# Scores and output projection of a gated cross-attention layer: three fp32r products each, or one plain fp32 product

## The chip, the cores and the metric

The kernel runs on one core of one Trainium2 chip. The metric is the device time of one execution in microseconds (us). All engines of the core run their own instruction streams and meet at semaphores: TensorE (PE in the profile, its weight loads PEld), VectorE (DVE), ScalarE (ACT), GpSimd (POOL) and SyncE (SP, which only issues transfers here).

## The reference, cut to what matters

Sixteen sequences of 256 tokens (width 256) attend to themselves and to 77 context rows, through 16 heads of 64; then comes a feed-forward part with a router, 15 experts and a shared branch.

```python
def xattn(image_embeds, latents, ...):            # x is (16, 256, 256), the context (16, 77, 256)
    x = layer_norm(image_embeds, ln1_g, ln1_b)
    l = layer_norm(latents, ln2_g, ln2_b)
    q = l @ Wq                                    # 256 x 1024
    k, v = split(concatenate([x, l], 1) @ Wkv)    # 333 keys per sequence
    w = softmax(einsum('bhqd,bhkd->bhqk', q * scale, k * scale))
    out = einsum('bhqk,bhkd->bhqd', w, v)
    return merge_heads(out) @ Wo                  # 1024 x 256
x = x + tanh(g_xattn[0]) * xattn(ctx_1024, layernorm(x), ...)
x = x + tanh(g_ffn[0]) * ffn(layernorm(x), ...)   # router top 2 of 16, experts, a causal convolution
```

## The kernel before

**Steps.** Attention is a software pipeline of 128 steps, 8 pairs of heads (`PAIRS`) in each of 16 sequences (`B`). A step `u` of sequence `b` does on TensorE, in this order: the scores of the pair of one step ago (`LAG_S`, L1396), probabilities times values of the pair of three steps ago (L1415), the projections of this pair's queries and keys (L1350, "Q" and "K"), the transposes of the normalised probabilities of two steps ago for the first two key tiles (`turned`, L1380), in six of eight steps one sixth of the value projection (L1350, "V", 512 columns), the third `turned`, in two of eight steps the transposes of the next sequence's rows (L1360, "L"), now and then work of the router, and the output projection of the pair of three steps ago (L1476), which adds up in the bank `yb` over eight pairs. Steps 0 to 31 and the last 16 are written out; the 80 between are a hardware loop of 16 steps, run five times (`pipeline`). The last sequences' router work, the shared branch and the experts follow, all of it in plain fp32.

**Precision.** Where a product must be as exact as fp32, the projections and two more products are made of three fp32r products: each operand is held as its rounded value and the rest (`Q_hl`, `K_hl`, `OT_hl`, `wo`, with an index of 0 or 1 for the two), and high times high, high times low and low times high are added in PSUM. The scores (L1396) and the output projection (L1476) are such products. Probabilities times values, all transposes and the feed-forward part are plain fp32 matmuls. The projections stay as they are in the change.

**Who makes the halves.** ScalarE copies a result bank to the rounded half (`Q_hl` at L1172, `K_hl` at L1180, `OT_hl` at L1168) and signals `q_hi`, `k_hi` or `ot_hi`; VectorE waits for that, subtracts and writes the other half (L1322, L1327, L1317), and it is this that releases the bank (`pj_free`) or tells TensorE (`ot_lo`). VectorE does this after the reciprocal of the sums (L1313), which waits for the fourth exponential, and before it copies two transposed tiles out of `st` (L1334, signal `pt_lo`). ScalarE copies the third (L1191, `pt_hi`). The scores need `pt_lo` and `pt_hi` of the step before, since they write the same `st` banks.

**Banks.** Q, K, V and L results take turns in two PSUM banks, `pj0` and `pj1`. So V, coming two fills after Q, goes into Q's bank and waits until that has been read.

**Output weights.** `Wo` is loaded to `stage` in two halves, each after one piece of the query weights has been split; in step 2 ScalarE copies (L1176) and GpSimd subtracts (L1100) to make `wo`. GpSimd's normalisation of probabilities (L1105, L1108) stands behind that in its stream.

**Shapes.** The scores take 64 rows: the two heads of a pair lie on partitions 0 to 63 and 64 to 127 and write different banks (`st_bank(2 * qt + head)`).

Of the kernel before, what the change touches and what calls it, by code (L numbers as in the profile page):

```python
# [587 lines left out]
def attention(nc, c, X, ident, tanh_g, kept, x, ctx_in, g_xattn, g_ffn, ln1_g, ln1_b, ln2_g, ln2_b,  # L588
# [53 lines left out]
    K_hl = sb("K_hl", [P, 2, 2, SKVE], F32R)  # L642
    Q_hl = sb("Q_hl", [P, 2, 2, SQ], F32R)
# [6 lines left out]
    OT_hl = sb("OT_hl", [P, 2, 2, SQ], F32R)  # L650
# [29 lines left out]
    with ExitStack() as weights:  # L680
        wq = weights.enter_context(nc.sbuf_tensor("wq", [P, 2, KD, INNER], F32R))
        wkv = weights.enter_context(nc.sbuf_tensor("wkv", [P, 2, KD, 2 * INNER], F32R))
        wo = weights.enter_context(nc.sbuf_tensor("wo", [P, 2, PAIRS, D], F32R))
# [13 lines left out]
    wo_in = [sem("wo_in0"), sem("wo_in1")]  # L697
    wo_hi = sem("wo_hi")
    wo_split = sem("wo_split")
# [15 lines left out]
    q_hi = sem("q_hi")  # L715
    k_hi = sem("k_hi")
# [9 lines left out]
    ot_hi = sem("ot_hi")  # L726
    ot_lo = sem("ot_lo")
# [53 lines left out]
    def st_bank(i):  # L781

        return st[i // 2][:, i % 2]
# [22 lines left out]

    def wo_half(i):
        return slice(i * PAIRS // 2, (i + 1) * PAIRS // 2)

    def wo_stage(i):  # L810
        return stage[:, i, :].rearrange("p (q d) -> p q d", d=D)
# [214 lines left out]
    def sync(sp):  # L1026
# [12 lines left out]
        for i in range(2):  # L1039
            sp.wait_ge(w_lo, i + 1)  # L1040
            sp.dma_start(wo_stage(i), Wo.rearrange("(q p) d -> p q d", p=P)[:, wo_half(i), :]
                         ).then_inc(wo_in[i], 16)
        sp.wait_ge(zeros_set, 3)

        def step(bb, u, has):
# [8 lines left out]
            if isinstance(bb, int) and bb == 0 and u == 4:  # L1054
                sp.wait_ge(wo_split, 2)
# [12 lines left out]
    def gpsimd(pool):  # L1068
# [22 lines left out]
        def step(bb, u, has):  # L1091
# [5 lines left out]
            if isinstance(bb, int) and bb == 0 and u == 2:  # L1097
                for i in range(2):
                    pool.wait_ge(wo_hi, i + 1)
                    pool.tensor_tensor(wo[:, 1, wo_half(i), :], wo_stage(i), wo[:, 0, wo_half(i), :].bitcast(F32),  # L1100
                                       ALU.subtract).then_inc(wo_split, 1)
# [36 lines left out]
    def scalar(act):  # L1138
# [13 lines left out]
        def step(bb, u, has):  # L1152
# [10 lines left out]
            if has(LAG_AV):  # L1163
# [4 lines left out]
                copy(OT_hl[:, v, 0, :], ov[:, 0:SQ], ACT.Copy).then_inc(ot_hi, 1)  # L1168
            if has(0):
                n, bank, _, _ = filled("Q", PAIRS, bb, u)  # L1170
                act.wait_ge(pj_full, n + 1)
                copy(Q_hl[:, r, 0, :], bank[:, 0:SQ], ACT.Copy, scale=SCALE).then_inc(q_hi, 1)  # L1172
            if isinstance(bb, int) and bb == 0 and u == 2:
                for i in range(2):
                    act.wait_ge(wo_in[i], 16)
                    copy(wo[:, 0, wo_half(i), :], wo_stage(i), ACT.Copy).then_inc(wo_hi, 1)  # L1176
            if has(0):
                n, bank, _, _ = filled("K", PAIRS, bb, u)
                act.wait_ge(pj_full, n + 1)
                copy(K_hl[:, r, 0, :], bank[:, 0:SKVE], ACT.Copy).then_inc(k_hi, 1)  # L1180
# [19 lines left out]
    def vector(dve):  # L1200
# [86 lines left out]
        def step(bb, u, has):  # L1287
# [26 lines left out]
            if has(LAG_AV):  # L1314
                m, v = PAIRS * bb + u - LAG_AV, (u - LAG_AV) % 2
                dve.wait_ge(ot_hi, m + 1)
                tt(OT_hl[:, v, 1, :], ov[:, 0:SQ], OT_hl[:, v, 0, :].bitcast(F32), ALU.subtract  # L1317
                   ).then_inc(ot_lo, 1)
            if has(0):
                _, bank, free, _ = filled("Q", PAIRS, bb, u)  # L1320
                dve.wait_ge(q_hi, PAIRS * bb + u + 1)
                nc.vector.scalar_tensor_tensor(Q_hl[:, r, 1, :], bank[:, 0:SQ], SCALE,  # L1322
                                               Q_hl[:, r, 0, :].bitcast(F32), ALU.mult, ALU.subtract
                                               ).then_inc(free, 1)
# [193 lines left out]
```

## Time and profile before

| what | value |
|---|---|
| three timed runs | 1327.8, 1330.31, 3483.99 us, median 1330.31 |
| profiled execution | 1328.71 us, span from first to last instruction 1327.0 us |
| mean granted TensorE clock | 0.990 |
| TensorE matmul / weight load busy | 1248.6 us (94%) / 1017.4 us (77%) |
| VectorE busy | 878.3 us (66%) |
| GpSimd busy | 740.0 us (56%) |
| ScalarE busy | 666.0 us (50%) |

The busy time of TensorE counts each matmul from its start to the modelled end of its pipeline, so consecutive matmuls overlap, and a short wait is hidden in it. What a matmul costs in a row of others is therefore read from start to start. A plain fp32 matmul leaves two records in the trace, an fp32r matmul and a transpose one. In the timeline, one row merges consecutive records of one group: its first number is the start of the first, its second the time to the last modelled end.

### The profile page before, as it was taken

Reading aid. Unit: us, or ns where it says so; the run is one execution under the profiler, and the core shown is the slowest. Engines: PE = TensorE matmul, PEld = TensorE weight load, DVE = VectorE, ACT = ScalarE, POOL = GpSimd, SP = SyncE. Lnnn points to the kernel's source line nnn. Section 1 sums busy time; section 2 is a strip of 40 time slices with the busy share of each in tenths; the row PEclk is TensorE's granted clock in tenths of the full one; section 3 lists DMA queues with packets and bytes.
Section 4 is the critical chain, followed back from the end, with each engine's and each line's share of the span. In section 5 each row is a group of like instructions: output and inputs, shape, how many; then the busy total and the mean of one; then the engine's idle time right before and its main releaser. Section 6 shows DMA issues by size and latency. Waiting matters only on the chain.

```text
span 1327.0 us, 28196 instructions
## 1 busy us (share of the span) xinstructions
PE 1248.6 (94%) x8982; PEld 1017.4 (77%) x8982; DVE 878.3 (66%) x2646; ACT 666.0 (50%) x2022; POOL 740.0 (56%) x894
## 2 busy tenths in 40 slices
PE   3899999999999999899999998999999989999996
PEld 2688787878787878788878787878788878787774
DVE  5566677777776777777767776777766656434554
ACT  3555555555544455455544554455545566454442
POOL 2655545656664666566646665666565642344555
PEclk9999999999998999999989999999999999999998
DMA  8910000000000000000000000000000070445666
GB/s 258 314 32 1 3 1 3 17 4 18 4 17 5 17 4 18 5 18 4 17 5 17 4 18 5 17 4 18 1 17 1 17 194 29 120 126 174 186 215 207
DMA packets 61839, 70.90 MB, mean 53 GB/s; under 512 B 7072, under 2 KB 56176, under 8 KB 61680
## 3 DMA queue, kind: packets, MB, share of 16 engines
q1 hardware_dynamic: 54192, 48.91, 12.7%
q0 software_dynamic: 6912, 18.95, 4.0%
q8 instruction: 84, 1.38, 0.5%
q10 hardware_dynamic: 576, 1.05, 0.2%
q14 instruction: 75, 0.61, 0.2%
HBM read 35.19 MB, written 33.70 MB: 52 GB/s over the span
## 4 chain that ended last, share of the span: by engine, by line
PE 37%; POOL 29%; issue 24%; DVE 6%; DMA 2%; ACT 1%; POOLq 0%; SPq 0%; DVEq 0%; ACTq 0%
POOL probs L1108 19%; PE pj L1350 9%; PE st L560 5%; PE ov L1415 4%; PE st L1396 4%; PE st L1380 4%; POOL probs L1105 3%; POOL slots_x L982 3%; PE pj L513 3%; PE ov L579 2%; PE yb L1476 2%; POOL rstd L1088 1%; PE st L550 1%; PE pj L516 1%; DVE PT L1334 1%
## 5 line engine op out<-in xcount | busy, mean ns | idle before, releaser
L1108 POOL TENSOR_SCALAR probs<-probs,inv_sum 128x333 f32<-128x333 f32 x384 | 425.7, 1125 | 0.0
L1160 ACT ACTIVATE probs<-st,neg_max 128x333 f32<-128x333 f32 x512 | 268.8, 538 | 275.0 <-DVE neg_max L1302 275.0
L1105 POOL TENSOR_TENSOR probs<-probs,inv_sum 128x333 f32<-128x333 f32 x128 | 94.8, 741 | 407.9 <-DVE inv_sum L1313 407.7
L1302 DVE TENSOR_REDUCE neg_max<-st 128x2 f32<-128x666 f32 x256 | 205.9, 846 | 134.6 <-PE st L1396 134.6
L1380 PE MATMUL st<-ident,probs 128*128 128x128 f32 (+1 forms) x1536 | 203.8, 272 | 1.1 <-POOL probs L1108 1.1
L1415 PE MATMUL ov<-PT,V 128*64 128x256 f32 (+1 forms) x1536 | 196.9, 392 | 0.0
L1380 PEld LDWEIGHTS st<-ident,probs 128*128 128x128 f32 (+1 forms) x1536 | 182.5, 143 | 17.3 <-POOL probs L1108 1.4
L1396 PE MATMUL st<-K_hl,Q_hl 64*128 64x334 f32 x1536 | 154.1, 332 | 19.0 <-issue 9.5
L1350 PE MATMUL pj<-wkv,lT 128*128 128x512 f32 (+1 forms) x576 | 158.4, 410 | 13.4 <-DVE Q_hl L1322 13.3
L1334 DVE COPY PT<-st 128x512 f32<-128x512 f32 x256 | 163.7, 681 | 0.8 <-PE st L1380 0.8
L1186 ACT ACTIVATE V<-pj 128x512 f32<-128x512 f32 (+1 forms) x96 | 57.3, 596 | 192.8 <-PE pj L1350 192.8
L1396 PEld LDWEIGHTS st<-K_hl,Q_hl 64*128 64x128 f32 x1536 | 119.7, 188 | 39.6 <-issue 24.2
L1415 PEld LDWEIGHTS ov<-PT,V 128*64 128x64 f32 (+1 forms) x1536 | 99.9, 138 | 64.5 <-issue 28.1
L1350 PE MATMUL pj<-lT,wkv 128*128 128x334 f32 x768 | 140.6, 319 | 0.6 <-DVE wkv L1275 0.6
L1350 PEld LDWEIGHTS pj<-lT,wq 128*128 128x128 f32 x768 | 100.7, 191 | 52.6 <-issue 49.3
L1350 PE MATMUL pj<-lT,wq 128*128 128x256 f32 x768 | 127.8, 302 | 3.0 <-DVE lT L1262 3.0
L1350 PEld LDWEIGHTS pj<-wkv,lT 128*128 128x128 f32 (+1 forms) x576 | 93.6, 175 | 47.5 <-DVE Q_hl L1322 20.3
L1476 PE MATMUL yb<-wo,OT_hl 128*128 128x256 f32 x768 | 122.5, 295 | 0.5 <-DVE OT_hl L1317 0.5
L1350 PEld LDWEIGHTS pj<-lT,wkv 128*128 128x128 f32 x768 | 119.5, 191 | 0.9 <-DVE wkv L1275 0.9
L1160 ACT ACTIVATION_READ_ACCUMULATOR probs<-st,neg_max 128x1 f32 x512 | 103.8, 203 | 0.0
L1476 PEld LDWEIGHTS yb<-wo,OT_hl 128*128 128x128 f32 x768 | 99.6, 190 | 0.8 <-DVE OT_hl L1317 0.8
L1191 ACT ACTIVATE PT<-st 77x512 f32<-77x512 f32 x128 | 75.1, 587 | 29.5 <-PE st L1380 29.5
(176 smaller groups left out, 1722.0 us busy)
## 6 DMA issues: line engine op xcount, KB each, us to landing
slots_x<-zeros SPq DMA_DIRECT2D x10, 1032.0 KB, 13.0
V<-slots_x SPq DMA_DIRECT2D x80, 129.0 KB
yg<-routed_y SPq DMA_DIRECT2D x32, 256.0 KB, 3.5
out<-X SPq DMA_DIRECT2D x32, 128.0 KB
X<-in_x SPq DMA_DIRECT2D x2, 1024.0 KB, 14.7
w_gu<-in_L_ffn_expert_gate_w SPq DMA_DIRECT2D x2, 960.0 KB, 9.1
w_gu<-in_L_ffn_expert_up_w SPq DMA_DIRECT2D x2, 960.0 KB, 10.3
w_dn<-in_L_ffn_expert_down_w SPq DMA_DIRECT2D x1, 1920.0 KB, 12.7
```

Source lines behind the costliest of these rows:

```text
L560: last = nc.tensor.matmul(pg[m % 2], xT[:, m % 2, k * P:(k + 1) * P], w_gu[:, bass.ds(e, 1), k].rearrange("p a g i -> p (a g i)"), start=( ...
L1105: pool.tensor_tensor(probs[:, v, 0, 0:SKV], probs[:, v, 0, 0:SKV], inv_sum[:, v, 0:1].to_broadcast([P, SKV]), ALU.mult).then_inc(normed, 1)
L1108: pool.tensor_scalar(probs[:, v, i, 0:SKV], probs[:, v, i, 0:SKV], inv_sum[:, v, i:i + 1], None, ALU.mult).then_inc(normed, 1)
L1160: nc.scalar.activation(probs[:, v, i, 0:SKV], st_bank(i)[:, 0:SKV], ACT.Exp, bias=neg_max[:, v, i:i + 1], accum_out=sums[:, v, i:i + 1]).t ...
L1191: copy(PT[0:kn, v, 2, :], st_bank(2)[0:kn, :], ACT.Copy).then_inc(pt_hi, 1)
L1302: nc.vector.tensor_reduce(neg_max[:, v, 2 * i:2 * i + 2], st[i][:, :, 0:SKV], AX.X, ALU.max, negate=True).then_inc(maxed, 1)
L1334: nc.vector.tensor_copy(PT[:, v, kt, :], st_bank(kt)).then_inc(pt_lo, 1)
L1350: last = mm(out, lhs(a, k), rhs(r, k), start=(k == 0 and i == 0), stop=(k == KD - 1 and i == 2))
L1380: last = nc.tensor.transpose(st_bank(kt)[0:kn, at:at + P], probs[:, v, i, k0:k0 + kn], ident[:])
L1396: last = mm(st_bank(2 * qt + head)[:, 0:SKVE], Q_hl[own, r, a, qt * P:(qt + 1) * P], K_hl[own, r, a_, :], start=(n == 0), stop=(n == 2))
L1415: last = mm(ov[half * HALF:(half + 1) * HALF, 0:SQ], V[0:kn, kt, head * DH:(head + 1) * DH], PT[0:kn, v, kt, half * SQ:(half + 1) * SQ], s ...
L1476: last = mm(yb[:, t * D:(t + 1) * D], OT_hl[:, v, a, t * P:(t + 1) * P], wo[:, r_, q, :], start=(q == 0 and t == 0 and i == 0), stop=(q == ...
```

## The change

Scores and output projection become single plain fp32 matmuls. `Q_hl`, `K_hl` and `OT_hl` become `Q`, `K` and `OT`, one fp32 value each. ScalarE copies Q (with the scale) and OT, and its Q copy releases the bank; VectorE copies K straight from the bank and releases it. The subtractions and ScalarE's K copy are gone. `wo` is one tile that one transfer of 1 MB fills, issued without a wait; the copies and subtractions of step 2 are gone.

```diff
-    K_hl = sb("K_hl", [P, 2, 2, SKVE], F32R)
-    Q_hl = sb("Q_hl", [P, 2, 2, SQ], F32R)
+    K = sb("K", [P, 2, SKVE])
+    Q = sb("Q", [P, 2, SQ])
...
-    OT_hl = sb("OT_hl", [P, 2, 2, SQ], F32R)
+    OT = sb("OT", [P, 2, SQ])
...
-        wo = weights.enter_context(nc.sbuf_tensor("wo", [P, 2, PAIRS, D], F32R))
+        wo = weights.enter_context(nc.sbuf_tensor("wo", [P, PAIRS, D], F32))
...
-        for i in range(2):
-            sp.wait_ge(w_lo, i + 1)
-            sp.dma_start(wo_stage(i), Wo.rearrange("(q p) d -> p q d", p=P)[:, wo_half(i), :]
-                         ).then_inc(wo_in[i], 16)
+        sp.dma_start(wo[:], Wo.rearrange("(q p) d -> p q d", p=P)).then_inc(wo_in, 16)
...
-                sp.wait_ge(wo_split, 2)
+                sp.wait_ge(w_lo, KD)
...
-            if isinstance(bb, int) and bb == 0 and u == 2:
-                for i in range(2):
-                    pool.wait_ge(wo_hi, i + 1)
-                    pool.tensor_tensor(wo[:, 1, wo_half(i), :], wo_stage(i), wo[:, 0, wo_half(i), :].bitcast(F32),
-                                       ALU.subtract).then_inc(wo_split, 1)
...
-                copy(OT_hl[:, v, 0, :], ov[:, 0:SQ], ACT.Copy).then_inc(ot_hi, 1)
+                copy(OT[:, v, :], ov[:, 0:SQ], ACT.Copy).then_inc(ot_ready, 1)
             if has(0):
-                n, bank, _, _ = filled("Q", PAIRS, bb, u)
+                n, bank, free, _ = filled("Q", PAIRS, bb, u)
                 act.wait_ge(pj_full, n + 1)
-                copy(Q_hl[:, r, 0, :], bank[:, 0:SQ], ACT.Copy, scale=SCALE).then_inc(q_hi, 1)
...
+                copy(Q[:, r, :], bank[:, 0:SQ], ACT.Copy, scale=SCALE).then_inc(free, 1)
...
-            if has(LAG_AV):
-                m, v = PAIRS * bb + u - LAG_AV, (u - LAG_AV) % 2
-                dve.wait_ge(ot_hi, m + 1)
-                tt(OT_hl[:, v, 1, :], ov[:, 0:SQ], OT_hl[:, v, 0, :].bitcast(F32), ALU.subtract
-                   ).then_inc(ot_lo, 1)
             if has(0):
-                _, bank, free, _ = filled("Q", PAIRS, bb, u)
-                dve.wait_ge(q_hi, PAIRS * bb + u + 1)
-                nc.vector.scalar_tensor_tensor(Q_hl[:, r, 1, :], bank[:, 0:SQ], SCALE,
-                                               Q_hl[:, r, 0, :].bitcast(F32), ALU.mult, ALU.subtract
-                                               ).then_inc(free, 1)
-                _, bank, free, _ = filled("K", PAIRS, bb, u)
-                dve.wait_ge(k_hi, PAIRS * bb + u + 1)
-                tt(K_hl[:, r, 1, :], bank[:, 0:SKVE], K_hl[:, r, 0, :].bitcast(F32), ALU.subtract
-                   ).then_inc(free, 1)
+                n, bank, free, _ = filled("K", PAIRS, bb, u)
+                dve.wait_ge(pj_full, n + 1)
+                nc.vector.tensor_copy(K[:, r, :], bank[:, 0:SKVE]).then_inc(free, 1)
...
                 for qt in range(QT):
-                    for n, (a, a_) in enumerate(((0, 0), (0, 1), (1, 0))):
-                        for head in range(2):
-                            own = slice(head * HALF, (head + 1) * HALF)
-                            last = mm(st_bank(2 * qt + head)[:, 0:SKVE], Q_hl[own, r, a, qt * P:(qt + 1) * P],
-                                      K_hl[own, r, a_, :], start=(n == 0), stop=(n == 2))
+                    for head in range(2):
+                        own = slice(head * HALF, (head + 1) * HALF)
+                        last = mm(st_bank(2 * qt + head)[:, 0:SKVE], Q[own, r, qt * P:(qt + 1) * P], K[own, r, :],
+                                  start=True, stop=True)
                     last.then_inc(st_full, 1)
...
-
-                    for i, (a, r_) in enumerate(((0, 0), (0, 1), (1, 0))):
-                        last = mm(yb[:, t * D:(t + 1) * D], OT_hl[:, v, a, t * P:(t + 1) * P], wo[:, r_, q, :],
-                                  start=(q == 0 and t == 0 and i == 0), stop=(q == PAIRS - 1 and i == 2),
-                                  skip_group_check=True)
+                    last = mm(yb[:, t * D:(t + 1) * D], OT[:, v, t * P:(t + 1) * P], wo[:, q, :],
+                              start=(q == 0 and t == 0), stop=(q == PAIRS - 1), skip_group_check=True)
```

TensorE's stream at the end of one step and the start of the next (step 4 of the first sequence, the third transposes to the values product of the next step), before; `waits` names the semaphores of a row:

```order
L1380 MATMUL st<-ident,probs 77x128 [waits exped]
L1380 MATMUL st<-ident,probs 77x128 x3
L1360 MATMUL pj<-ident,z 128x128 [waits pj_free0,rows_ready]
L1360 MATMUL pj<-ident,z 128x128
L1361 MATMUL pj<-ident,z 128x77
L1476 MATMUL yb<-wo,OT_hl 128x256 [waits ot_lo]
L1476 MATMUL yb<-wo,OT_hl 128x256 x5
L1396 MATMUL st<-K_hl,Q_hl 128x334 [waits pt_lo,pt_hi,exped,pj_free0]
L1396 MATMUL st<-K_hl,Q_hl 128x334 x11
L1415 MATMUL ov<-PT,V 64x256 [waits pt_hi,pt_lo,ot_lo]
```

The same place of the changed kernel:

```order
L1342 MATMUL st<-ident,probs 77x128 [waits exped]
L1342 MATMUL st<-ident,probs 77x128 x3
L1322 MATMUL pj<-ident,z 128x128 [waits pj_free0,rows_ready]
L1322 MATMUL pj<-ident,z 128x128
L1323 MATMUL pj<-ident,z 128x77
L1436 MATMUL yb<-wo,OT 128x256 [waits ot_ready]
L1436 MATMUL yb<-wo,OT 128x256
L1358 MATMUL st<-K,Q 128x334 [waits pt_lo,exped,pt_hi,pj_free0,pj_free1]
L1358 MATMUL st<-K,Q 128x334 x3
L1377 MATMUL ov<-PT,V 64x256 [waits pt_hi,pt_lo,ot_ready]
```

The output projection has two matmuls in place of six and the scores four in place of twelve; the order of the groups is the same, and the scores wait for both banks' readers.

VectorE's stream in a step with row work, from the score maxima to the next maxima, before:

```order
L1302 TENSOR_REDUCE neg_max<-st 128x2 [waits st_full] x2
L1313 RECIPROCAL inv_sum<-sums 128x4 [waits exped]
L1317 TENSOR_TENSOR OT_hl<-ov,OT_hl 128x256 [waits ot_hi]
L1322 SCALAR_TENSOR_TENSOR Q_hl<-pj,Q_hl 128x256 [waits q_hi]
L1327 TENSOR_TENSOR K_hl<-pj,K_hl 128x334 [waits k_hi]
L1334 COPY PT<-st 128x512 [waits pt_full] x2
L1251 TENSOR_SCALAR lT<-pj,gb 128x256 [waits pj_full]
```

and of the changed kernel:

```order
L1275 TENSOR_REDUCE neg_max<-st 128x2 [waits st_full] x2
L1286 RECIPROCAL inv_sum<-sums 128x4 [waits exped]
L1290 COPY K<-pj 128x334 [waits pj_full]
L1296 COPY PT<-st 128x512 [waits pt_full] x2
L1224 TENSOR_SCALAR lT<-pj,gb 128x256 [waits pj_full]
```

Three subtractions between the reciprocal and the copies of PT have become one copy, which waits for TensorE and no longer for ScalarE.

## Rows read from the trace of the kernel before

**Rows 1.** The page: busy us (share) xinstructions, and shares of the chain:
```profile
PE 1248.6 (94%) x8982; PEld 1017.4 (77%) x8982; DVE 878.3 (66%) x2646; ACT 666.0 (50%) x2022; POOL 740.0 (56%) x894
...
PE 37%; POOL 29%; issue 24%; DVE 6%; DMA 2%; ACT 1%; POOLq 0%; SPq 0%; DVEq 0%; ACTq 0%
```

**Rows 2.** Busy time in windows: stretch, length, then PE, PEld, DVE, ACT, POOL, clock, DMA:
```profile
48.00:1066.00 1018.00, 990.39 (x7639) 812.07 (x7637) 720.45 (x2081) 520.63 (x1618) 604.40 (x666) 0.99 0.05 17
```

**Rows 3.** Waits of TensorE, whole run: waiting line, awaited: us, times, longest:
```profile
PE pj L1350 <- DVE Q_hl L1322: 13.3, 27, 2.0
PE st L1396 <- issue: 9.5, 4, 2.5
PE st L1396 <- DVE PT L1334: 6.8, 16, 1.7
```

**Rows 4.** Timeline: start us, us to modelled end, engine, line, operation; PE, one step:
```profile
486.00 1.03 PE L1380 MATMUL st<-ident,probs 128*128 128x128 f32 x8
486.86 1.66 PE L1350 MATMUL pj<-wkv,lT 128*128 128x512 f32 x6
488.35 0.60 PE L1380 MATMUL st<-ident,probs 128*77 128x128 f32 x4
488.79 0.38 PE L1004 MATMUL ov<-ident,h_send 128*128 128x128 f32 x2
488.93 0.97 PE L1476 MATMUL yb<-wo,OT_hl 128*128 128x256 f32 x6
489.82 1.19 PE L1396 MATMUL st<-K_hl,Q_hl 64*128 64x334 f32 x12
490.94 1.52 PE L1415 MATMUL ov<-PT,V 128*64 128x256 f32 x12
492.39 0.99 PE L1350 MATMUL pj<-lT,wq 128*128 128x256 f32 x6
493.21 1.10 PE L1350 MATMUL pj<-lT,wkv 128*128 128x334 f32 x6
494.15 1.04 PE L1380 MATMUL st<-ident,probs 128*128 128x128 f32 x8
```

**Rows 5.** Timeline of TensorE, a step without a value projection:
```profile
504.90 0.96 PE L1476 MATMUL yb<-wo,OT_hl 128*128 128x256 f32 x6
505.90 1.19 PE L1396 MATMUL st<-K_hl,Q_hl 64*128 64x334 f32 x12
```

**Rows 6.** Timeline of TensorE in the shared branch, plain fp32 and full array:
```profile
1102.13 1.03 PE L527 MATMUL yb<-w_sd,gated 128*128 128x256 f32 x4
1102.99 0.38 PE L1004 MATMUL ov<-ident,h_send 128*128 128x128 f32 x2
```

**Rows 7.** Timeline 493 to 497, the bank of Q: who reads it, who waits:
```profile
493.81 0.41 ACT L1172 ACTIVATE Q_hl<-pj 128x256 fp32r<-128x256 f32 x1
...
494.78 0.39 DVE L1317 TENSOR_TENSOR OT_hl<-ov,OT_hl 128x256 fp32r<-128x256 f32 x1
...
495.09 0.41 DVE L1322 SCALAR_TENSOR_TENSOR Q_hl<-pj,Q_hl 128x256 fp32r<-128x256 f32 x1
495.42 0.50 DVE L1327 TENSOR_TENSOR K_hl<-pj,K_hl 128x334 fp32r<-128x334 f32 x1
...
495.56 1.61 PE L1350 MATMUL pj<-wkv,lT 128*77 128x512 f32 x6 [0.37 <-DVE Q_hl L1322]
...
495.83 1.28 DVE L1334 COPY PT<-st 128x512 f32<-128x512 f32 x2
```

**Rows 8.** Timeline of the start, steps 2 and 3 of the first sequence:
```profile
41.30 4.70 POOL L1100 TENSOR_TENSOR wo<-stage,wo 128x1024 fp32r<-128x1024 f32 x2 [2.00 <-ACT wo L1176]
...
50.05 1.53 PE L1380 MATMUL st<-ident,probs 128*128 128x128 f32 x12 [1.09 <-POOL probs L1108]
```

**Rows 9.** Groups by form, weight loads: times count, busy us, mean ns of one:
```profile
L1396 PEld LDWEIGHTS st<-K_hl,Q_hl 64*128 64x128 f32 x1536 | 119.7, 188 | 39.6 <-issue 24.2 <-DVE PT L1334 5.3
...
L513 PEld LDWEIGHTS pj<-hT,w_cv 128*128 128x128 f32 x192 | 35.9, 193 | 6.7 <-issue 2.0
```

More of the change, by code:

```diff
@@ L696, in attention @@
     w_in = [sem(f"w_in{i}") for i in range(3 * KD)]
-    wo_in = [sem("wo_in0"), sem("wo_in1")]
-    wo_hi = sem("wo_hi")
-    wo_split = sem("wo_split")
+    wo_in = sem("wo_in")
     w_hi = sem("w_hi")
@@ L714, in attention @@
     pj_free = [sem(f"pj_free{i}") for i in range(len(pj))]
-    q_hi = sem("q_hi")
-    k_hi = sem("k_hi")
     st_full = sem("st_full")
@@ L725, in attention @@
     ov_full = sem("ov_full")
-    ot_hi = sem("ot_hi")
-    ot_lo = sem("ot_lo")
+    ot_ready = sem("ot_ready")
     y_full = sem("y_full")
@@ L805, in known @@
         return not isinstance(v, int) or v >= 1
[L807 to L811, printed above, removed]
     def tiles_of(t, j):
@@ L1167, in step @@
                     act.wait_ge(y_full, m - 1)
-                copy(OT_hl[:, v, 0, :], ov[:, 0:SQ], ACT.Copy).then_inc(ot_hi, 1)
+                copy(OT[:, v, :], ov[:, 0:SQ], ACT.Copy).then_inc(ot_ready, 1)
             if has(0):
-                n, bank, _, _ = filled("Q", PAIRS, bb, u)
+                n, bank, free, _ = filled("Q", PAIRS, bb, u)
                 act.wait_ge(pj_full, n + 1)
-                copy(Q_hl[:, r, 0, :], bank[:, 0:SQ], ACT.Copy, scale=SCALE).then_inc(q_hi, 1)
[L1173 to L1180, printed above, removed]
+                copy(Q[:, r, :], bank[:, 0:SQ], ACT.Copy, scale=SCALE).then_inc(free, 1)
             if p in V_STEPS and has(0):
@@ L1384, in step @@
                 m, r = PAIRS * bb + u - LAG_S, (u - LAG_S) % 2
-                _, _, kfree, kvalue = filled("K", PAIRS, bb, u - LAG_S)
-                pe.wait_ge(kfree, kvalue + 1)
+                for kind in ("Q", "K"):
+                    _, _, free, value = filled(kind, PAIRS, bb, u - LAG_S)
+                    pe.wait_ge(free, value + 1)
                 if known(m):
@@ L1401, in step @@
                 if known(m):
-                    pe.wait_ge(ot_lo, m)
+                    pe.wait_ge(ot_ready, m)
                 route_columns_free(pe, bb, u, has)
@@ L1452, in step @@
             if has(LAG_Y):
-                pe.wait_ge(ot_lo, PAIRS * bb + u - LAG_Y + 1)
+                pe.wait_ge(ot_ready, PAIRS * bb + u - LAG_Y + 1)
             if turns_conv:
@@ L1471, in step @@
                 if isinstance(m, int) and m == 0:
-                    pe.wait_ge(wo_split, 2)
+                    pe.wait_ge(wo_in, 16)
                 for t in range(QT):
-                    for i, (a, r_) in enumerate(((0, 0), (0, 1), (1, 0))):
-                        last = mm(yb[:, t * D:(t + 1) * D], OT_hl[:, v, a, t * P:(t + 1) * P], wo[:, r_, q, :],
-                                  start=(q == 0 and t == 0 and i == 0), stop=(q == PAIRS - 1 and i == 2),
-                                  skip_group_check=True)
+                    last = mm(yb[:, t * D:(t + 1) * D], OT[:, v, t * P:(t + 1) * P], wo[:, q, :],
+                              start=(q == 0 and t == 0), stop=(q == PAIRS - 1), skip_group_check=True)
                 last.then_inc(y_full, 1)
@@ L1496, in attention @@
         pj_full=pj_full, ov_full=ov_full, y_full=y_full, y_read=y_read, exped=exped, pt_lo=pt_lo, pt_hi=pt_hi,
-        ot_lo=ot_lo, h_rows=h_rows, slots_clear=slots_clear)
+        ot_ready=ot_ready, h_rows=h_rows, slots_clear=slots_clear)
 _INS = ["x", "ctx_1024", "g_xattn", "g_ffn", "L0_xattn_ln1_g", "L0_xattn_ln1_b", "L0_xattn_ln2_g",
```

## The prediction, made before the changed kernel was run

> **What bounds the kernel now.** I read the page first: TensorE is busy 94% of the span, VectorE 66%, GpSimd 56%, ScalarE 50% [rows 1]. Then the busy time in the window that holds attention: 990.4 of 1018 us [rows 2]. So at most some 28 us of visible idle time stand there, and a step's length is the sum of TensorE's groups. The view of waits says what the idle time is: the value projection waiting for the bank that VectorE's second half of Q releases (13.3 us, 27 times, the start included), the scores waiting for VectorE's copies of PT (6.8 us), and 9.5 us "issue" in four waits of the scores, one at each of four of the loop's turns [rows 3]. Matmul ends are modelled, so I price work from start to start in the timeline: what must be seen there is the pitch of each kind of matmul and what a group costs beyond its pitch.
>
> **Pitches.** Four plain fp32 records of 256 columns take 1102.99 - 1102.13 = 0.86 us, 0.216 each, and a plain matmul is two records [rows 6]. Six fp32r matmuls of 256 columns (Q) take 492.39 to 493.21, 0.82, with one exposed weight load in it; six of 334 columns (K) take 493.21 to 494.15, 0.94, so 0.155 each [rows 4]. So per result a plain product has two records of about twice the length of one fp32r matmul: four units against three. The halves of a transition matter too: the twelve scores run as six simultaneous pairs, 489.82 to 490.94 = 1.12 us, of which 6 x 0.155 = 0.93 is streaming and 0.19 is the first weight load and the change of array shape. The values product, plain fp32 with the two heads side by side in columns, takes 490.94 to 492.39 = 1.45, 6 x 0.216 = 1.30 plus 0.15 [rows 4]. That row also shows that plain fp32 pairs on two parts of the array do run at once.
>
> **Output projection.** Before: two transposes and the projection, 488.79 to 489.82, 1.03 us [rows 4]. Changed: the transposes at 0.109 each (four transposes took 488.79 - 488.35 = 0.44) 0.22, four records 0.86, and about 0.09 to change to the 64-row shape (the part of the 0.15 and 0.19 above that stands at an end; estimated as half of them): 1.17. That is +0.14 to +0.15 per step, x 128 = **+19 us**. The 0.14 us between 488.79 and 488.93 shows why the projection's own 0.89 may not be compared with 0.86: an fp32r group starts 0.08 early in the record and pays it at its first matmul.
>
> **Scores.** No row shows plain fp32 on 64 rows with 334 columns. A record would take 0.216 x 334 / 256 = 0.282; four matmuls are eight records, four pairs, 1.13 us, plus a surplus between 0.15 (values product, plain but with 64-column weights) and 0.19 (present scores, 128-column weights): 1.28 to 1.32. I take 1.30, +0.18 per step, x 128 = **+23 us** (20 to 26). Together TensorE gets 42 us more to do. Nothing hides this: TensorE is the engine that is not idle.
>
> The Trainium skill has a rule that speaks against the change here: "TensorE: Matmul & The Clock Gate", section "Weight-path perf modes", says that fast weight loading is on for 128 weights when the input type is not FP32, so plain fp32 would lose it. The trace does not bear it out: a load for the fp32r scores takes 188 ns, one for the plain convolution 193 [rows 9]. As a mechanism of this kernel: if the plain load took twice the time, one more exposed load, about half the scores' surplus of 0.19, would be paid per step, +12 us; all other loads would still lie under records of 0.216 or more.
>
> **Waits that go.** (a) V waits for Q's bank. In the step of [rows 7] ScalarE has read Q at 494.22, VectorE releases the bank at 495.50, and V starts at 495.56 although the eight transposes from 494.15 [rows 4] would have let it start at 494.15 + 0.79 = 494.94 (eight at 0.109, less the 0.08 of above). The wait is 0.62; the view gives 0.37, so each of the 27 printed waits is short by about 0.25. In the step before, 486.00 to 486.86 is 0.86 where 0.79 would do: a wait of 0.07 that no view prints, and there are 69 such value projections (6 of 8 steps, 96 in all). 13.3 + 27 x 0.25 + 69 x 0.07 = 25; allowing for some that are printed in full I take 24 us. With the change ScalarE's copy releases the bank. It ends 0.7 us before TensorE could use it in this step, so nothing is late next but after a loop turn; I leave 1.5 us. **-22.5 us.** (b) Scores wait for PT. 6.8 us are printed. Unprinted: 504.90 to 505.90 is 1.00 where 0.89 would do [rows 4, 5]. I take 0.04 on average over 128 steps, 5 us, 12 us in all. VectorE now does one copy (I price it at the 0.50 us of the K subtraction, a bound from above) in place of three operations from 494.78 to 495.92 [rows 7], so PT is copied 0.6 us earlier; also the output projection, which stands between the transposes and the scores, is 0.15 longer, and that part of the wait is covered by the longer work that I have already charged. **-11.5 us.** What would be late next is ScalarE's copy of the third tile, in some steps. (c) At the start GpSimd's 4.7 us of splitting Wo stand ahead of the normalisation, and TensorE waits 1.09 us for it [rows 8]. **-1 us.** Sum of the waits: -35, bounds -20 (the printed ones alone) and -41.
>
> **At nothing.** VectorE loses about 0.8 us and ScalarE one 0.45 us copy per step; neither is full. K's release: VectorE's copy comes after the reciprocal, as before, and the next fill of that bank is a step away or behind V and the last transposes. The scores' new wait for Q's bank stands a step behind ScalarE's copy; queued behind it are the values product and the next projections, and none is delayed. SyncE issues Wo in one transfer, at the end of its weight loads, without two waits; the transfers behind it (clearing of slots, rest of x) move earlier, and the conv weights' wait is met by then. The loop's turns stay, 9.5 us.
>
> **Sum.** 1328.7 (the profiled execution; span 1327.0) + 19 + 23 - 35 = 1335.7. The profiled run stands 1.6 us under the median of the runs shown, 1330.3. I forecast **1336 us**: TensorE's extra passes and the waits saved nearly cancel. From here on, 2% either way (1303.7 and 1356.9) is about what a measurement of this kernel can tell from no change.
>
> **Rivals.**
> 1. *Row pairs of plain fp32 do not overlap.* Then the eight records of the scores are paid one by one, 8 x 0.282 + 0.19 = 2.45, +1.33 per step, 170 us in place of 23: 1483. Against: fp32r row pairs and plain column pairs both overlap [rows 4]. Chance 8%.
> 2. *The waits are replaced.* ScalarE's copy of Q stands behind four exponentials and the OT copy, and where these are late V waits for them; if only 10 of the 35 us come back, 1361, slower. Against: Q is read 0.7 us before the need [rows 4, 7]. It decides from 14 us or less saved. 10%.
> 3. *The other side: not TensorE but the loop of maxima, exponentials, normalisation and transposes is the bound.* The chain of waits gives GpSimd 29% [rows 1]. Then the extra 42 us fall into idle time of TensorE and the shorter VectorE part, 35 us, is won in full: 1294, faster. It would need as much idle time on TensorE as it hides; there are 28 us [rows 2], and GpSimd makes TensorE wait once [rows 8]. It decides where more than 32 of the 42 us are hidden. 5%.
> 4. *The weight load costs double*: 1348. The skill's rule named above would bring it; the load rows speak against. 5%.
> 5. *The granted clock moves.* It stands at 0.99 in the attention window [rows 2]; each 1% more or less on TensorE-bound stretches is 10 us: 1326 to 1346. It goes with the forecast.
>
> **How the numbers follow.** Forecast with its clock variants 72%, rivals 8, 10, 5 and 5. Within 2% are the forecast and rival 4, 77%; slower are rivals 1 and 2, 18%; faster rival 3, 5%. The forecast's own bounds are 1328.7 + 39 - 41 = 1327 and 1328.7 + 45 - 20 = 1354, with 10 us of clock on the lower side 1317. Leaving out rival 1, rival 3 and part of rival 2 leaves 80% in 1318 to 1359.
>
> **What would show it.** Scores from start to start: 1.30 us in the changed trace (2.45 by rival 1, 1.40 by rival 4), about 0.28 between pairs. Output projection with two transposes ahead: 1.17. Transposes to V: 0.87, no wait on Q. VectorE's share falls from 66% to about 58%, TensorE's idle time in attention to little more than the loop's turns. It would be wrong if the scores' step is far from 1.30, or if the waits' view lists ScalarE's Q copy or PT copy with over 10 us.

## The result and the profile after

| | before | changed |
|---|---|---|
| median | 1329.1 us | 1346.6 us |
| runs that stand for it | 1325.4 to 1330.3 | 1345.9 to 1354.0 |
| ratio to before | | 1.0149 (95% interval 1.0133 to 1.0164) |
| profiled execution | 1328.7 | 1354.0 |
| mean granted clock there | 0.990 | 0.982 |

I forecast 1336 us. The change is slower by 17.5 us, and the measured time lies 10.6 us above the forecast. One run of before, at 3484 us, and one of e10 below, at 1401.5 us with a clock of 0.946, are left out of the ratios; the median of 1329.1 still counts the first and is 1328.4 without it. The changed kernel's profiled execution is 7 us longer than its median run; the other four have a clock of 0.990, so differences read in this profile are too large by about that much.

The page of the changed kernel, busy us, share and instructions, and the chain's shares:

```profile
PE 1290.4 (95%) x8214; PEld 981.1 (73%) x8214; DVE 797.7 (59%) x2390; ACT 611.0 (45%) x1892; POOL 735.0 (54%) x892
...
PE 91%; issue 2%; DVE 2%; DMA 2%; ACT 1%; POOL 1%; SPq 0%; DVEq 0%; POOLq 0%; ACTq 0%
```

VectorE's share fell from 66% to 59%. The chain that ended last, which ran over TensorE for 37% and GpSimd for 29% [rows 1], now is TensorE's for 91%. A chain is one path among several that may be nearly as long; the idle time says it better. In the window of attention (same columns as [rows 2]) TensorE is idle 14.4 us of 1040, where it was 28 of 1018:

```profile
48.00:1088.00 1040.00, 1025.61 (x6854) 772.70 (x6856) 639.80 (x1826) 467.17 (x1488) 597.25 (x661) 0.98 0.05 14
```

Its waits, whole run:

```profile
PE st L1358 <- issue: 14.0, 8, 2.0
...
PE pj L1312 <- ACT Q L1153: 1.2, 2, 1.1
...
PE st L1358 <- ACT PT L1164: 0.8, 1, 0.8
...
PE st L1358 <- DVE PT L1296: 0.4, 1, 0.4
```

Against [rows 3]: the wait for Q's bank is 1.2 us instead of 13.3, the one for VectorE's PT copies 0.4 instead of 6.8. But "issue" before the scores has grown from 9.5 us in four waits to 14.0 in eight. An ordinary step, TensorE alone:

```profile
492.15 0.38 PE L993 MATMUL ov<-ident,h_send 128*128 128x128 f32 x2
492.36 1.03 PE L1436 MATMUL yb<-wo,OT 128*128 128x256 f32 x4
493.32 1.40 PE L1358 MATMUL st<-K,Q 64*128 64x334 f32 x8
494.65 1.52 PE L1377 MATMUL ov<-PT,V 128*64 128x256 f32 x12
496.10 0.97 PE L1312 MATMUL pj<-lT,wq 128*128 128x256 f32 x6
496.91 1.08 PE L1312 MATMUL pj<-lT,wkv 128*128 128x334 f32 x6
497.83 1.03 PE L1342 MATMUL st<-ident,probs 128*128 128x128 f32 x8
498.62 1.63 PE L1312 MATMUL pj<-wkv,lT 128*77 128x512 f32 x6
```

Scores 493.32 to 494.65, 1.33 us (median of all steps 1.324) against 1.12 [rows 4]; transposes and projection 492.15 to 493.32, 1.17 against 1.03; transposes before V 497.83 to 498.62, 0.79, which is what they need without a wait, against 0.86 and 1.41 [rows 4, 7]. The first two are as forecast within 0.03 us. For the third the prediction has two values, 0.79 where it works out the wait and 0.87 in its list of signs (eight at 0.109, without the 0.08 us by which the fp32r group behind them starts early); 0.79 is right. What was not forecast is at a turn of the loop:

```profile
541.06 1.03 PE L1436 MATMUL yb<-wo,OT 128*128 128x256 f32 x4
541.26 0.59 ACT L1164 ACTIVATE PT<-st 77x512 f32<-77x512 f32 x1 [1.52 <-PE st L1342]
544.11 0.29 PEld L1358 LDWEIGHTS st<-K,Q 64*128 64x128 f32 x3 [2.42 <-issue]
544.14 0.80 PE L1358 MATMUL st<-K,Q 64*128 64x334 f32 x2 [2.05 <-issue]
546.81 2.38 PE L1358 MATMUL st<-K,Q 64*128 64x334 f32 x6 [1.87 <-issue]
```

TensorE stops twice: 2.05 us before the scores and 1.87 us inside them, after three weight loads and two matmuls. No semaphore or transfer of the program is waited for. The clock falls there too, here in windows (length, busy of PE, PEld, DVE, ACT, POOL, granted clock, DMA):

```profile
541.00:544.00 3.00, 1.09 (x7) 0.64 (x4) 0.68 (x2) 0.59 (x1) 2.67 (x3) 1.00 0.03 8
544.00:547.00 3.00, 0.99 (x4) 0.49 (x6) 0.00 (x0) 0.00 (x0) 0.00 (x0) 0.64 0.04 11
547.00:549.00 2.00, 2.00 (x6) 0.97 (x5) 0.85 (x1) 0.00 (x1) 0.00 (x0) 0.50 0.04 8
549.00:553.00 4.00, 4.00 (x18) 2.37 (x18) 3.17 (x14) 2.64 (x9) 0.07 (x1) 0.50 0.00 2
```

TensorE was busy 2.1 of the 6 us from 541 to 547; then the work runs at half clock (0.50, the 1.2 GHz level). This profile has a half-clock stretch behind each of the four turns (6.8 or 10.2 us long); before, behind two of four. Adding up, group by group, what the groups at the four turns take over their usual length, a turn costs some 7.0 to 8.4 us in the changed kernel, about 30 us in all, and about 17 us in all before.

Sums over all groups from start to start, before and changed profile, worked out from the trace (us):

```
scores                              145.1   184.1   +39.0   (26 is their own price, 13 lies at the turns)
transposes of probabilities         181.0   161.6   -19.4
projection, with the router's and
 next rows' transposes before it    153.0   156.2    +3.2
everything else                     847.9   850.3    +2.4
```

### The profile page after: what moved, and what is told of

It is laid out like the page before. It is cut to its first block, busy times and chain, and to the rows that moved or that the text cites. A ratio compares the mean times of both kernels' runs of the same rounds, so it can differ in the third digit from the quotient of the medians.

```text
span 1352.2 us, 26237 instructions
## 1 busy us (share of the span) xinstructions
PE 1290.4 (95%) x8214; PEld 981.1 (73%) x8214; DVE 797.7 (59%) x2390; ACT 611.0 (45%) x1892; POOL 735.0 (54%) x892
## 3 DMA queue, kind: packets, MB, share of 16 engines
q8 instruction: 81, 1.33, 0.4%
## 4 chain that ended last, share of the span: by engine, by line
PE 91%; issue 2%; DVE 2%; DMA 2%; ACT 1%; POOL 1%; SPq 0%; DVEq 0%; POOLq 0%; ACTq 0%
PE pj L1312 27%; PE ov L1377 14%; PE st L1358 13%; PE st L1342 12%; PE yb L1436 8%; PE st L560 5%; PE pj L513 3%; PE ov L579 2%; PE st L550 1%; PE pj L516 1%; PE ov L1001 1%; PE yb L527 1%; DMA yg<-routed_y 1%; PE st L572 1%; PE ov L993 1%
## 5 line engine op out<-in xcount | busy, mean ns | idle before, releaser
L1358 PE MATMUL st<-K,Q 64*128 64x334 f32 x1024 | 185.6, 474 | 15.2 <-issue 14.0
L1358 PEld LDWEIGHTS st<-K,Q 64*128 64x128 f32 x1024 | 92.8, 188 | 81.5 <-issue 57.5
L1436 PE MATMUL yb<-wo,OT 128*128 128x256 f32 x512 | 135.3, 387 | 0.0
L1312 PEld LDWEIGHTS pj<-lT,wkv 128*128 128x128 f32 x768 | 120.6, 193 | 0.9 <-DVE wkv L1248 0.9
L1436 PEld LDWEIGHTS yb<-wo,OT 128*128 128x128 f32 x512 | 87.4, 191 | 6.8 <-ACT OT L1149 0.2
```

The costliest lines, as they stand in the source:

```text
L1312: last = mm(out, lhs(a, k), rhs(r, k), start=(k == 0 and i == 0), stop=(k == KD - 1 and i == 2))
L1358: last = mm(st_bank(2 * qt + head)[:, 0:SKVE], Q[own, r, qt * P:(qt + 1) * P], K[own, r, :], start=True, stop=True)
L1436: last = mm(yb[:, t * D:(t + 1) * D], OT[:, v, t * P:(t + 1) * P], wo[:, q, :], start=(q == 0 and t == 0), stop=(q == PAIRS - 1), skip_gro ...
```

## The experiments

The open question was where the 10 us beyond the forecast come from; theory 1 said the loop's turns, theory 2 the plain matmuls themselves or a clock that they pull down. Then each term of my sum was to be priced by itself.

**Padding, e1.** The code is moved, and nothing else is changed:

```diff
         pe.wait_ge(consts, 5)
+        for _ in range(16):
+            pe.wait_ge(tables, 1)
```

> The changed kernel with 16 already met waits more in TensorE's stream while it idles before its first matmul (about 1 us that nothing needs, TensorE waits to 15.6 us there). They do no work; they only move the loop's code by 16 instructions. Theory 1 (the 10 us beyond my forecast come from the loop's turns: in the changed trace TensorE stops twice at each of the four turns, about 2.0 us before the scores and 1.9 us inside them after their first few instructions, and the clock drops behind it at every turn; before it stopped once, 2.5 us): the place of the second stop is one of code position, so it goes away or moves, and the time falls by 6 to 14 us, to 1333 to 1341 us. Theory 2 (the longer plain matmuls themselves, or a clock that falls because of them): nothing changes, 1346 us, and the second stop stays.

Measured 1349.1 us, ratio 1.0170 (1.0151 to 1.0188): no gain. But the stop moved. TensorE at the same turn:

```profile
542.06 1.03 PE L1436 MATMUL yb<-wo,OT 128*128 128x256 f32 x4
548.04 2.60 PE L1358 MATMUL st<-K,Q 64*128 64x334 f32 x8 [4.95 <-issue]
```

and the sum over its four turns, in the view of waits, where the changed kernel has 14.0 us in eight:

```profile
PE st L1358 <- issue: 19.2, 4, 4.9
```

The two stops have become one of 4.95 us. So the second stop does hang on the place of the code, as theory 1 said, but 16 instructions brought no saving, as theory 2 said. The expectation of 1333 to 1341 was wrong; the question stayed open for larger shifts.

**Without a loop, e2 and e3.** In the changed kernel and in that of before:

```diff
-        for n in range(2 * UNROLL):
-            written_out(n)
-        with eng.Fori(0, (N - 3 * UNROLL) // UNROLL) as i:
-            for u in range(UNROLL):
-                step(2 * i + 4, u, lambda lag: True)
-        for n in range(N - UNROLL, N):
+        for n in range(N):
             written_out(n)
```

> The changed kernel with its 80 loop steps written out, so that no turn of a loop is left. Theory 1: the turns cost 30 us in the profiled run (excess over the usual length of the groups at the four turns, the clock's part included) and about 23 in the median run, so 1346.6 - 23 = 1324 us (1316 to 1328). Theory 2: turns cost the same 10 to 17 us in both kernels, so 1332 us or more. In the trace the scores should take 1.32 us and the projection with two transposes ahead 1.18, as with the loop.

> The kernel before with its 80 loop steps written out. Its turns cost 17 us in the profiled run (2.5 us stop each, and in two of four a stretch at half clock behind it). Theory 1: 1329 - 16 = 1313 us (1309 to 1317), and the distance to the changed kernel written out the same way is 8 to 12 us: 26 for the scores and 19 for the projection less 35 of waits. Theory 2: 1313 too, but the distance stays 17 us.

Measured 1323.6 us (0.9969, 0.9957 to 0.9981) and 1314.2 us (0.9906, 0.9888 to 0.9924). Both lie in the ranges of theory 1, and in e2 the scores take 1.32 us and the projection with two transposes 1.18. The turns cost the changed kernel 23 us and the kernel before 14 us (it took 1327.7 us in the same round of runs); without them the change costs 9.3 us (8.4 by the two ratios), inside the 8 to 12 of theory 1. The window from 48 us to the last scores of e2 (same columns as [rows 2]):

```profile
48.00:1059.00 1011.00, 1009.92 (x6864) 764.20 (x6862) 636.53 (x1826) 466.68 (x1488) 600.10 (x661) 1.00 0.05 14
```

TensorE is idle 1 us of 1011, and the clock is 1.00 throughout: plain fp32 matmuls in a dense stream do not pull it down. Theory 2 falls. The sums from start to start of e3 and e2 give the bare terms: scores +25.7 us, transposes of probabilities -14.3 (the wait for Q's bank), the projection with the router's and next rows' transposes before it +2.1 net of the waits that it covers, the rest -4.3. The wait for Q's bank, counted over the 94 groups of transposes that stand before V, each above the 0.79 us that it needs, is 21.2 us in the kernel before, 15.6 in e3 and 0.5 in e2: the loop had a part in it.

**Larger padding, e8, e9, e11, e12.** The edit of e1 with 128 (e8, and e9 timed), 64 and 192 in place of 16.

> The changed kernel with 128 met waits in place of 16 in TensorE's idle start. With 16 the two stops of a turn (2.0 and 1.9 us) became one of 4.9 us before the scores, and the time stayed. Theory 1a: a turn costs the fetch of as many blocks of code as lie between the loop's start and the point that is already there, and with another position that is one block less: one stop of about 2.5 us, 1335 to 1341 us. Theory 1b: the cost does not depend on the position: stops of 4 to 5 us in all per turn, 1347 to 1352 us.

> The same kernel as e8_pad128 (the changed one with 128 met waits in TensorE's idle start), timed: theory 1a, the place of the loop's code decides what a turn costs: 1334 to 1340 us, a ratio of 1.003 to 1.008 to the kernel before. Theory 1b, the one look was chance: 1346.

> The changed kernel with 64 waits in place of 16 or 128. Theory 1a: between the two: stops at the turn of either about 5 us (1345 to 1350 us) or about 2 (1335 to 1340 us), nothing between, if whole blocks of code are what is waited for. A rival, that the stop shrinks evenly with the number of waits: about 3.5 us per turn, 1343.

> The changed kernel with 192 waits. If blocks of code matter, the cost of a turn goes in a cycle: with 128 it was low, with 0 and 16 high. I expect 192 low as well or back at the high value, no third value: 1335 to 1340 or 1345 to 1352 us. A rival, that more waits ahead are always better: below 1335.

Measured: e8 1336.9 us in one run; e9 1337.3 us, ratio 1.0076 (1.0057 to 1.0095); e11 1332.0 and e12 1332.7, one run each (their stated intervals began at 1335). The turn in e9's timeline of TensorE:

```profile
537.18 1.03 PE L1436 MATMUL yb<-wo,OT 128*128 128x256 f32 x4
539.96 1.40 PE L1358 MATMUL st<-K,Q 64*128 64x334 f32 x8 [1.75 <-issue]
```

The "issue" row in the waits of e11, four stops:

```profile
PE st L1358 <- issue: 7.2, 4, 2.1
```

With 64, 128 and 192 there is one stop of 1.5 to 2.1 us per turn, and three of the four turns have no half-clock stretch behind them; with 0 and 16 the stops at a turn come to 3.3 to 4.95 us, and every turn has such a stretch. Counted over the groups as above, the four turns cost some 28 us in e1 and 9 in each of e9, e11 and e12. So where the loop's code lies decides between a dear turn and a cheap one: 1332.0 to 1337.3 us against 1346.6 and 1349.1, of which the 1332.0 and 1332.7 are single runs. The rival "shrinks evenly" falls: 64 waits do as much as 192. The times of e11 and e12 lie below my intervals, and e12's in that of its rival, "more waits ahead are always better: below 1335"; the rival falls only because 64 waits gave 1332.0 and 128 gave 1337.3. Those 5 us between e9 and the other two are no matter of the turns. In e9 the scores wait four times more, once behind each turn by 34 to 36 us, for VectorE's copy of PT, and each time VectorE itself had waited 4.0 to 4.5 us for a scatter of the router's rows (at most 2.8 us in e11 and e12). The row of e9's view of waits, and the first of these places in its timeline:

```profile
PE st L1358 <- DVE PT L1296: 5.4, 4, 1.6
...
438.07 0.17 DVE L918 TENSOR_SCALAR h_send<-h_send 128x2 f32<-128x2 f32 x1 [4.02 <-DMA slots_x<-h_send,slot_i]
```

```profile
q8 instruction: 3, 0.05, 1.7%
...
q8 instruction: 3, 0.05, 1.6%
...
q8 instruction: 2, 0.03, 1.0%
...
q8 instruction: 1, 0.02, 0.4%
```

Between turns a piece comes about every 16 us, and in e2 and e3 no two start nearer than 13.7 us from 300 to 1000 us. At the turn above, the changed kernel's three start at 540.6, 544.2 and 548.4 us. The first has landed at 542.0, as the stop begins, and TensorE goes on at 544.14. The second starts then, but TensorE needs it after two more matmuls: it has landed at 545.3, and TensorE goes on at 546.81. In e9 the first has landed at 537.9, TensorE goes on at 539.96, and the second, started then, is not waited for. It is the same at every turn: where there is one short stop (28 turns in seven kernels), TensorE goes on 1.9 to 2.2 us behind the landing of the first piece; the changed kernel and e1 need the second too and go on 1.3 to 1.9 us behind its landing. So theory 1a stands: a turn costs the wait for one 16 KB piece of TensorE's code or for two, by where the loop's code lies. That it is these transfers that release the stops is read from their times at 36 turns; the profile names no releaser. What the place must be is open, since I tried five of them, and so is whether the cost goes in a cycle.

**The same on the kernel before, e10.**

> The kernel before with the same 128 waits. If the place of the code decides in any kernel, its turns change too, either way: by a stop of 2 us and a clock's fall at each of four turns the most, 1322 to 1344 us, and the stops before the scores are not 2.5 us any more. If it is something of the changed kernel alone: 1329 us and four stops of 2.5 us.

Measured 1331.0 us, ratio 1.0025 (1.0015 to 1.0036). The stops in its view of waits:

```profile
PE st L1396 <- issue: 8.6, 4, 2.3
```

Four stops with 8.6 us in place of four with 9.5 [rows 3], each 2.1 to 2.3 us long where they were 2.1 to 2.5, and a little slower in time. The kernel before already waited for only one piece of code at a turn, and so it stayed; neither alternative of the expectation is clearly met. It gained nothing and lost 3.3 us, which I can't put to a group; it has five half-clock stretches of 3.4 us ahead of the last one, three of them behind turns.

**Each half of the change alone, e5 and e6**, both on e2. In e5 the scores go back to three fp32r products, with the halves of Q and K made as before; the core of the edit:

```diff
-                    for head in range(2):
-                        last = mm(st_bank(2 * qt + head)[:, 0:SKVE], Q[own, r, qt * P:(qt + 1) * P], K[own, r, :],
+                    for n, (a, a_) in enumerate(((0, 0), (0, 1), (1, 0))):
+                        for head in range(2):
+                            last = mm(st_bank(2 * qt + head)[:, 0:SKVE], Q_hl[own, r, a, qt * P:(qt + 1) * P],
+                                      K_hl[own, r, a_, :], start=(n == 0), stop=(n == 2))
```

In e6 it is the projection, with the halves of OT and Wo made as before:

```diff
-                    last = mm(yb[:, t * D:(t + 1) * D], OT[:, v, t * P:(t + 1) * P], wo[:, q, :],
+                    for i, (a, r_) in enumerate(((0, 0), (0, 1), (1, 0))):
+                        last = mm(yb[:, t * D:(t + 1) * D], OT_hl[:, v, a, t * P:(t + 1) * P], wo[:, r_, q, :],
```

> The changed kernel written out (e2_after_flat, 1323.6 us), with the scores alone back to three fp32r products and their halves made as before; the output projection stays plain. By my terms: 0.205 us less per step, 26 us, but V waits for VectorE's release of Q's bank again (15.5 us in e3_before_flat) and the scores for PT a little (2 to 4 us, since the longer projection covers most of it): 1323.6 - 26 + 15.5 + 3 = 1316 us (1312 to 1320). If the price of the scores were hidden in waits, no change: 1323.

> The changed kernel written out, with the output projection alone back to three fp32r products (with its split of Wo at the start); scores and their copies stay plain. By my terms: 0.15 us less per step, 19 us; given back 1 to 2 us at the start (GpSimd's split of Wo) and up to 3 where TensorE waits for VectorE's half of OT: 1323.6 - 19 + 3 = 1308 us (1304 to 1312). A rival: OT's second half is needed within the same step and takes back more than half: 1314 or more.

Measured 1311.7 us (0.9867, 0.9850 to 0.9885) and 1317.5 us (0.9910, 0.9893 to 0.9926). With e2 and e3 this is a full table, all without a loop:

```
                     projection fp32r    projection plain
scores fp32r         1314.2 (e3)         1311.7 (e5)
scores plain         1317.5 (e6)         1323.6 (e2)
```

Plain scores cost 12 us beside the plain projection and 3 us beside the split one; the plain projection gains 2.5 us beside split scores and costs 6 beside plain ones. The table mixes two rounds of runs, in which the kernel before took 1327.7 us (e2, e3) and 1329.1 (e5, e6). By the ratios to it plain scores cost 13.5 and 0.5 us, and the plain projection gains 5 and costs 8, so the small prices are known to some 3 us only; that plain scores cost much more beside the plain projection holds either way. The four prices differ because the two parts pay with the same waits. From start to start, V's wait for Q's bank is 15.6 us in e3, 4.0 in e5 and 0.5 in e6 and e2: either part of the change removes most of it. What stands between the projection and the scores beyond the usual length is 15.8, 9.4, 6.2 and 2.8 us in that order. Two rows of e5's view of waits:

```profile
PE st L1365 <- DVE PT L1303: 6.8, 19, 1.0
...
PE pj L1319 <- DVE Q_hl L1291: 4.5, 4, 2.0
```

The wait for Q's bank, in the loopless kernel before 15.6 us from start to start, is 4.0 there, although VectorE still makes Q's second half: without the subtraction of OT ahead of it VectorE comes in time at all but 17 of 94 places. I had expected the full 15.5 back (1316, bounds 1312 to 1320; the measured time is below them). In e6 the expected 1304 to 1312 was missed the other way. I had charged the projection's 19 us as if no wait came back, and of 19 us won the groups show only 13.3 (projection 8.1, the router's and next rows' transposes ahead of it 3.6, transposes of probabilities directly ahead of it 1.6): the shorter projection uncovers the waits for PT again, 3.5 us more between it and the scores, and the start gives back a 2.1 us wait for GpSimd, which splits Wo. The rival of that expectation, a time of 1314 or more, came true in its size, but not for its reason: waits for OT's second half are 3.2 us in all.

**Only the release of Q's bank, e4 and e7.** The kernel before, with a loop (e4) and without (e7):

```diff
+    Q32 = sb("Q32", [P, 2, SQ])
...
+                if p in V_STEPS:
+                    copy(Q32[:, r, :], bank[:, 0:SQ], ACT.Copy, scale=SCALE).then_inc(q_full, 1)
+                    copy(Q_hl[:, r, 0, :], bank[:, 0:SQ], ACT.Copy, scale=SCALE).then_inc(free, 1)
...
+                if p in V_STEPS:
+                    dve.wait_ge(free, value + 1)
+                    tt(Q_hl[:, r, 1, :], Q32[:, r, :], Q_hl[:, r, 0, :].bitcast(F32), ALU.subtract)
```

> The kernel before, three fp32r products everywhere, with one thing of the change in another form: in the six of eight steps that have a value projection, ScalarE copies Q twice out of the bank (once in fp32 to a new tile, once rounded) and its second copy releases the bank; VectorE subtracts from the fp32 copy. It prices the waits of V by themselves. If the change's waits are worth what I took, 22.5 us for V, the time is 1329 - 22 = 1307 us (1303 to 1312), 2 or 3 more if K's later rounded copy makes the copies of PT later in the steps without V. The rival, that the wait is only replaced (V then waits for ScalarE, or the scores for PT): 1322 us or more.

> e4_bank_early written out. e4 took V's waits away whole (the transposes before V take 0.79 us again) and gave back 8 us in 14 waits of the router's logits for the second half of OT. Against e3_before_flat (1314.2 us): 15.5 less, 8 more: 1307 us (1302 to 1310). A rival, in which the turns of the loop made e4's gain look small and there is no giving back: 1299.

Measured 1315.7 us (0.9914, 0.9893 to 0.9934) and 1304.9 us (0.9829, 0.9803 to 0.9855). V's wait is gone but for little in both: the transposes before it take 0.79 us (median), and their excess, 21.2 us in the kernel before, is 2.4 us in e4 and 0.9 in e7. e4 gained 12 us and not 22, above the 1303 to 1312 that I had stated, because 8 us came back at once in a place that the change does not have: in the steps with router work the logits stand behind the wait for OT's second half, and 14 times TensorE now came too early for it. The view of that line in e4 counts 24 records, the weight load and the matmul of 12 of them:

```profile
L1013 PE MATMUL ov<-w_rt,h_turned x128: 179/263/375, 174.4 to 1099.2; 128*128 128x16 f32 x128
its engine sat idle before it (us, times) until:
  DVE OT_hl L1322: 14.9, 24
```

The loopless e7 was expected at 1307 (1302 to 1310) and came at 1304.9. It is 1.7% faster than the kernel before and 3.1% faster than the changed one, and keeps the precision scheme of before.

## Why the prediction was right or wrong

**Right: what bounds it, and the price of the passes.** The four units against three showed as read from the rows: the projection with two transposes took 1.17 us, forecast 1.17; the scores 1.32, forecast 1.30. The step that was a little short is "I take 1.30" between 1.28 and 1.32: the group's first interval and its last carry 0.10 us each over the pitch, so the upper end (the surplus 0.19 of the present scores) was right, and the scores cost 26 us, not 23. Rival 1 (row pairs do not overlap) is out, the pairs start 7 ns apart. So is rival 4 (doubled load), which would have made the scores 1.40: a plain fp32 load for the scores takes 188 ns, like the fp32r one [rows 9]. Rival 3, a faster kernel, needed 32 of the 42 us hidden in TensorE's idle time, and the kernel is slower.

**Right: the waits that go.** V's wait, 24 us by my estimate and 21.2 from start to start, fell to 0.7. The scores' waits for PT fell to 0.4 us printed. Rival 2 is out. Against my sum of 7 us stands the loopless difference of 9.3, but that they lie so near is in part luck: without a loop the scores cost 2.7 us more than I took and V's wait gave back 8 us less, while the projection, with 2.1 us net where I had 19 - 11.5, and the rest gave back 9 us more.

**Wrong: "The loop's turns stay, 9.5 us."** I took over the printed stops of before as a constant, in the paragraph on what costs nothing, and named no cover or condition for it. The changed kernel has 24 records of matmuls and weight loads in a step's two groups where there were 36, so all later code lies elsewhere. TensorE then needs two pieces of its code at a turn where one had been enough, and its printed stops are 14.0 us in place of 9.5 at four turns. The rest came from the clock behind it: I had put the granted clock down as a matter of its own that "goes with the forecast" (rival 5), symmetric around it. It was not symmetric: behind the longer stops it fell at every turn. By medians, turns cost 14 us before (e3) and 23 us in the changed kernel (e2); these 9 us are most of the 10.6 by which the forecast was low, and with cheap turns the changed kernel measured 1332 to 1337 us (e9, e11, e12), around the forecast of 1336. Even that is not the forecast come true term by term: these turns cost some 9 us, less than the 14 to 17 of the kernel before, which the sum had left as they were.

**The verdict.** The range, 1318 to 1359, holds the time. The likeliest case, that the passes and the waits nearly cancel, was not what was measured: the kernel is slower by 1.3% to 1.6%, clear of its noise, though short of the 2% that I had called slower. The two parts of the change interact through the waits (e5, e6), which my sum could not show: it gave each wait to one part.

## What to carry to other kernels

Three fp32r products against one plain fp32 product came here to three passes against four on TensorE (the scores took 1.12 us and 1.32), plus the work of the halves elsewhere; where TensorE is the bound, look first whether the waits that the halves cause can be removed without giving up the cheaper passes (here an early release of the bank, 12 us, and loopless code, 11 to 14 us, gave 1.7% together). Price waits that two edits share in a table of both, since the second edit finds them already paid. And when a change alters the number of instructions ahead of or in a loop, its turns are no constant: count the instruction transfers at a turn, and compare versions written out, or at several positions of the code, before a per cent is put down to the change.

## What the runs showed of the hardware

- A turn of TensorE's loop stops it for 1.5 to 2.5 us or for 3.3 to 5 us, and the same kernel went from one to the other by 64, 128 or 192 instructions that do nothing. No transfer or semaphore of the program releases the stop; a 16 KB transfer of instructions on q8 lands 1.9 to 2.2 us before the end of the shorter ones, and for the longer ones a second lands 1.3 to 1.9 us before the end.
- Behind the long stops the clock fell to half at all eight turns (changed kernel, e1), for 3.4 to 10.2 us; behind stops near 2 us at three of twelve (e9, e11, e12), and behind those of 2.1 to 2.5 us of the kernel before at two of four, in e10 at three of four.
- A subtraction of 128 x 256 on VectorE took twice as long in e4 when both sources lay in SBUF: with one source in a PSUM bank (its L1322, OT) 398 ns, with both in SBUF 869 ns, medians. In 93 of the 96 GpSimd was at work for over nine tenths of the time, and these took 424 to 1081 ns; the other three took 386, 395 and 426 ns. In the kernel before, the subtraction of Q with one source in a bank took 405 to 425 ns beside a GpSimd as busy (125 of 128). So contention with GpSimd is the likely reason, though only three cases stand on the other side:

```profile
L1329 DVE TENSOR_TENSOR Q_hl<-Q,Q_hl x96: 386/869/1081, 26.8 to 1043.1; 128x256 fp32r<-128x256 f32 x96
```

- Plain fp32 on 64 rows runs two heads at once like fp32r: pairs 7 ns apart, 0.281 us per pair of records of 334 columns. An fp32r group behind a plain one is recorded 0.08 us early and pays it at its first matmul, so groups of the two kinds can only be compared with their neighbours.
